# Five dense attentions: stacked q and k through device memory, and a new order of their pipeline

## What is computed

```python
# context_attention_0 (154 keys, a mask row), causal_attention_1 (512 keys, causal)
# remembered_attention_1 (154 keys), context_attention_2 (154 keys, a mask per query)
scores = einsum('bhqd,bhkd->bhqk', q, k) / sqrt(8)       # masked where the part has a mask
out = einsum('bhqk,bhkd->bhqd', softmax(scores), v)
# differential_attention_2 (512 keys): two softmaxes over two pairs of q and k
wei = softmax(q1 @ k1.T / sqrt(8)) - lamb * softmax(q2 @ k2.T / sqrt(8))
```

## Time and profile before

| | us |
|---|---|
| median of 3 runs (5172.68 to 5182.78) | 5179.9 |
| span of the profiled execution | 5172.1 |
| busy: PE, DVE, ACT, POOL | 4078.9, 3239.9, 2680.8, 1243.4 |
| attend, context 0 (482 to 661) | 179 |
| attend, causal (855 to 1120) | 265 |
| attend, remembered (1202 to 1382) | 180 |
| attend, differential, first and second (1529 to 1797, 1799 to 2066) | 268, 267 |
| attend, context 2 (2135 to 2328) | 193 |

### The profile page before, as it was taken

One profiled execution on the slowest core, in us unless ns is written; L12 is line 12 of the kernel. 1 busy time (PEld: TensorE's weight loads), 2 busy tenths in 40 slices (PEclk: granted clock), 3 DMA queues, 4 the chain that ended last, 5 costly groups with the idle time before them and its releaser, 6 DMA issues. The chain is left out here.

```text
span 5172.1 us, 126690 instructions
## 1 busy us (share of the span) xinstructions
PE 4078.9 (79%) x45549; PEld 2392.3 (46%) x45678; DVE 3239.9 (63%) x5957; ACT 2680.8 (52%) x5510; POOL 1243.4 (24%) x2886
## 2 busy tenths in 40 slices
PE   2004767876668888596997579999999999999997
PEld 1003333332332222243443337777777777777775
DVE  7996444544437676534555327777777777777775
ACT  2034723554547667361224436666666666666665
POOL 0011200111201111110000134444444444444443
PEclk6557977987879999796998679999999999999998
DMA  2000020000010000002441000000000000000000
GB/s 57 0 0 1 2 69 23 1 1 1 1 33 2 1 2 1 11 1 57 140 137 51 5 23 28 6 10 24 6 28 6 6 28 6 10 24 6 28 6 11
DMA packets 60833, 110.22 MB, mean 21 GB/s; under 512 B 11399, under 2 KB 43251, under 8 KB 59164
## 3 DMA queue, kind: packets, MB, share of 16 engines
q1 hardware_dynamic: 59558, 101.70, 6.8%
q0 software_dynamic: 784, 1.80, 0.2%
HBM read 96.06 MB, written 1.74 MB: 19 GB/s over the span
## 5 line engine op out<-in xcount | busy, mean ns | idle before, releaser
L676 DVE TENSOR_REDUCE minus_max<-banks 128x1 f32<-128x512 f32 (+4 forms) x1152 | 605.7, 569 | 320.7 <-PE banks L571 314.4
L641 ACT ACTIVATE probs<-banks 128x512 f32<-128x512 f32 (+4 forms) x1152 | 581.1, 557 | 339.0 <-PE banks L609 336.6
L2961 POOL TENSOR_TENSOR loc_cos_part<-loc_cos_part,loc_sin_part 128x512 f32<-128x512 f32 x388 | 494.3, 1274 | 672.0 <-DVE loc_sin_part L3390 671.4
L3034 PE MATMUL banks<-loc_w_qkv,loc_shifted 128*128 128x256 f32 x1552 | 391.4, 395 | 15.4 <-DMA loc_adder_of<-loc_head_ones 15.4
L609 PE MATMUL banks<-q_stack,k_stack 64*128 64x512 bf16 (+3 forms) x1152 | 255.3, 382 | 97.1 <-DMA q_stack<-max_rows 69.6
L3423 DVE TENSOR_TENSOR loc_headsT<-banks,loc_sum_inv 128x512 f32<-128x512 f32 x192 | 132.5, 690 | 291.5 <-ACT loc_sum_inv L3295 291.5
L3034 PEld LDWEIGHTS banks<-loc_w_qkv,loc_shifted 128*128 128x128 f32 x1552 | 282.1, 192 | 55.0 <-DMA loc_w_qkv<-in_L_ffn_Wqkv_dram 15.7
L622 PE MATMUL banks<-probs,pair_rows 128*32 128x512 f32 (+3 forms) x2304 | 295.5, 589 | 0.0
L3415 DVE TENSOR_REDUCE loc_minus_max<-banks 128x4 f32<-128x384 f32 x386 | 196.9, 551 | 153.3 <-PE banks L3101 152.5
L700 POOL CAST max_parts<-minus_max 128x8 bf16<-128x8 f32 x192 | 36.4, 189 | 1043.2 <-DVE minus_max L676 1043.2
L1987 PE MATMUL banks<-identity,srt_b 128*128 128x128 f32 x64 | 11.3, 321 | 344.4 <-DVE srt_b L2267 344.4
(11 more groups left out here) (524 smaller groups left out, 9305.9 us busy)
## 6 DMA issues: line engine op xcount, KB each, us to landing
expert_share<-limited_rows SPq DMA_DIRECT2D x136, 256.0 KB, 3.9
expert_w<-in_L_ffn_pairs_dram SPq DMA_DIRECT2D x84, 192.0 KB, 2.3
loc_w_qkv<-in_L_ffn_Wqkv_dram SPq DMA_DIRECT2D x7, 1536.0 KB, 8.3
expert_share<-grouped_rows SPq DMA_DIRECT2D x32, 256.0 KB, 4.0
q_stack<-max_rows SPq DMA_DIRECT2D x384, 3.0 KB
loc_v_edge<-loc_v SPq DMA_DIRECT2D x192, 32.0 KB, 1.8
fixed_w<-in_L_ffn_experts_dram SPq DMA_DIRECT2D x8, 514.5 KB, 3.7
loc_pack<-in_L_ffn_pack_dram SPq DMA_DIRECT2D x6, 537.5 KB, 4.0
```

Source lines behind the costliest of these rows:

```text
L641: nc.scalar.activation(probs[(a % 2) * C + k][e][0:kn, q0:S], t_bank[e][0:kn, q0:S], ACT.Exp, scale=scale).then_inc(s["exp_done"], 1)
L676: nc.vector.tensor_reduce(minus_max[:, u, e, qs[0]:qs[0] + len(qs)], view, AX.X, ALU.max, negate=True).then_inc(s["max_done"], 1)
L2961: nc.gpsimd.tensor_tensor(cos_part[:, tiles, :], cos_part[:, tiles, :], sin_part[:, tiles, :], ALU.add).then_inc(s["summed"], 1)
L3034: ins = nc.tensor.matmul(g.bank[3 * j][:, (t % 2) * QK:(t % 2 + 1) * QK], xs[:, t * P:(t + 1) * P], w_qkv[:, ds(at, QK)], start=True, stop ...
```

## The change

- A class `Stacks` owns two q and two k stacks of a whole batch (8 pairs each) and, per pair of projections, two tensors in device memory, 128 x 6 x (4 batches of keys or queries), bf16. `store` writes a batch there in six DMAs (pieces repeated as the six slots want them), `load` fetches a batch in four, with heads and slots laid on 48 rows of each half. `project` gains an SP program that stores each batch as it is ready and loads the first two, and a GpSimd program that sets the stacks to 1.0 before. The second q and k of the differential part are stored at its end.
- The selection matrices, their products, the copies to `q_stack` and `k_stack` and the patterns go. A key bias gets its own row by two DMAs per batch; the row of maxima lies behind it.
- `attend` is unrolled for 32 pairs, with no hardware loop. Direct runs 3 pairs ahead (4 with 154 keys), the maxima are sent 2 ahead, from two buffers. Three banks serve the turned scores and three the direct ones. The unit on TensorE is one turned product of half e and one direct product of half 1-e; values come in halves of the queries at set places between the units, turning of rows and heads too. Masks come unit by unit. Products read only the rows and keys that are used (51 or 52 rows, 26 keys in the second key tile).
- SP loads the batch after next when a batch has been used up. GpSimd copies value rows into a double buffer.
- The first part loads neither `select_q` nor `select_k` nor the patterns, and computes no `stack_ones`.

```diff
+    def store(self, sp, i, first, count, sem):
+        q_parts, k_parts = self.parts[i]
+        q_dram, k_dram = self.drams[i]
+        q = slice(first * S, (first + count) * S)
+        k = slice(first * self.nk, (first + count) * self.nk)
+        for slots, pieces in ((slice(0, 3), slice(0, 3)), (slice(3, 5), slice(0, 2)), (slice(5, 6), slice(0, 1))):
+            sp.dma_start(q_dram[:, slots, q], q_parts[:, pieces, q]).then_inc(sem, 16)
+        for slots, piece in ((slice(0, 3), 0), (slice(3, 5), 1), (slice(5, 6), 2)):
+            n = slots.stop - slots.start
+            sp.dma_start(k_dram[:, slots, k], k_parts[:, piece:piece + 1, k].to_broadcast(
+                [P, n, count * self.nk])).then_inc(sem, 16)
+    def load(self, sp, batch):
+        i, b = divmod(batch, B)
+        for e in range(2):
+            rows = slice(64 * e, 64 * e + MAX_ROW)
+            for stacks, dram, n in ((self.q, self.drams[i][0], S), (self.k, self.drams[i][1], self.nk)):
+                src = dram.rearrange("(a e d) s t -> e (d s) a t", e=2, d=DH)[e][:, :, b * n:(b + 1) * n]
+                sp.dma_start(stacks[batch % 2][rows, :, :], src).then_inc(self.s[f"loaded{batch % 2}"], 16)
+    def load_bias(self, sp, batch, key_bias):
+        for e in range(2):
+            row = 64 * e + MAX_ROW
+            src = key_bias[0:1, batch:batch + 1, 0:self.nk].to_broadcast([1, PAIRS, self.nk])
+            sp.dma_start(self.k[batch % 2][row:row + 1, :, :], src).then_inc(self.s[f"bias_loaded{batch % 2}"], 16)
+def project(nc, g, projections, values, stacks):
...
+            @block.sync
+            def _(sp):
+                for b in range(B):
+                    sp.wait_ge(s["third_ready"], b * n + 2)
+                    stacks.store(sp, 0, b, 1, stacks.s[f"stored{b}"])
+                    if b == 0:
+                        sp.wait_ge(stacks.s["stacks_filled"], 4)
+                    if b in (1, 2):
+                        sp.wait_ge(stacks.s[f"stored{b - 1}"], 96)
+                        stacks.load(sp, b - 1)
+                if n > 2:
+                    sp.wait_ge(s["third_ready"], B * n)
+                    stacks.store(sp, 1, 0, B, stacks.s["stored_later"])
+            @block.gpsimd
+            def _(pool):
+                for buffer in (*stacks.k, *stacks.q):
+                    nc.gpsimd.memset(buffer[:, :, :], 1.0).then_inc(stacks.s["stacks_filled"], 1)
...
-    LAG = 2 if n_kt > 2 else 1
-    RING = 4
-    QUAD = PAIRS // 2
+    N, QUADS = B * PAIRS, B * PAIRS // 2
+    AHEAD = 4 if context else 3
+    SENT_AHEAD = 2
+    max_row = stacks.max_row
+    VALUES_OWN = {7: (0, 0)} if context else {13: (0, 0), 14: (0, 1)}
+    VALUES_NEXT = ({1: (0, 1), 2: (1, 0), 3: (1, 1)} if context else
+                   {1: (1, 0), 3: (1, 1), 5: (2, 0), 6: (2, 1), 7: (3, 0), 9: (3, 1)})
+    ROWS_AT = (1, 5) if context else (4, 12)
+    COPY_ROWS_AT = (2, 6) if context else (5, 13)
+    COPY_HEADS_AT = 4 if context else 11
+    TURN_HEADS_AT = 6 if context else 15
 
...
+        def load_next(sp, b):
+
+            batch = which * B + b + 2
+            if batch >= B * len(stacks.parts):
+                return
+            sp.wait_ge(s["turned_ready"], (b + 1) * PAIRS * 2 * C)
+            if batch // B:
+                sp.wait_ge(stacks.s["stored_later"], 96)
+            else:
+                sp.wait_ge(stacks.s[f"stored{batch}"], 96)
+            stacks.load(sp, batch)
...
+                for n in range(N):
+                    sp.wait_ge(s["rows_done"], n + 1)
+                    for e in range(2):
+                        row = 64 * e + max_row
+                        sp.dma_start(stacks.q[batch_of(n) % 2][row:row + 3, n % PAIRS, :],
+                                     max_rows[n % 2][3 * e:3 * e + 3, :]).then_inc(s[f"sent{n % 2}"], 16)
+                    b, a = divmod(n, PAIRS)
+                    if a == 2 and b:
+                        load_next(sp, b - 1)
+                load_next(sp, B - 1)
 
...
+                def turned(n, k, e):
+                    q_stack, k_stack = stacks_of(n)
+                    k0, kn = ktiles[k]
+                    q0 = k0 if causal else 0
+                    rows_e = slice(64 * e, 64 * e + max_row + 3)
+                    if k == 0 and e == 0:
+                        pe.wait_ge(s[f"sent{n % 2}"], 32 * (n // 2 + 1))
+                    if plain:
+                        after(pe, "exp_done", unit(n, k, e) - 2)
+                    nc.tensor.matmul(t_bank(n, k, e)[0:kn, q0:S], k_stack[rows_e, k0:k0 + kn], q_stack[rows_e, q0:S],
+                                     start=plain, stop=True, skip_group_check=True).then_inc(s["turned_ready"], 1)
...
+                def slot(n):
+                    quad = n // 2
+                    ahead = n + AHEAD
                     for k in range(C):
+                        for i in range(2):
+                            if not plain:
+                                turned_masks(n, k, i)
+                                if ahead < N:
+                                    direct_masks(ahead, k, i)
+                            turned(n, k, i)
+                            if ahead < N:
+                                direct(ahead, k, i)
+                            at = place(n, k, i)
+                            if at in VALUES_NEXT and quad:
+                                attend_values(quad - 1, *VALUES_NEXT[at])
+                            if at in VALUES_OWN:
+                                attend_values(quad, *VALUES_OWN[at])
+                            if at in ROWS_AT and n + SENT_AHEAD < N:
+                                turn_rows(n + SENT_AHEAD)
+                            if at == TURN_HEADS_AT and quad:
+                                turn_heads(quad - 1)
+                for n in range(AHEAD):
+                    for k in range(C):
+                        for i in range(2):
+                            if not plain:
+                                direct_masks(n, k, i)
+                            direct(n, k, i)
+                    if 0 < n <= SENT_AHEAD:
+                        turn_rows(n - 1)
+                for n in range(N):
+                    slot(n)
+                for piece in VALUES_NEXT.values():
+                    attend_values(QUADS - 1, *piece)
+                turn_heads(QUADS - 1)
...
+                def exp(n, k, e):
+                    k0, kn = ktiles[k]
+                    q0 = k0 if causal else 0
+                    quad, u = n // 2, n % 2
+                    act.wait_ge(s["turned_ready"], unit(n, k, e) + 1)
+                    after(act, "values_done", (quad - copies[u]) * C + k + 1)
+                    nc.scalar.activation(probs_of(n, k, e)[0:kn, q0:S], t_bank(n, k, e)[0:kn, q0:S], ACT.Exp,
+                                         scale=scale).then_inc(s["exp_done"], 1)
+                def copy_rows(n):
+                    act.wait_ge(s["max_turned"], n + 1)
+                    after(act, f"sent{n % 2}", 32 * (n // 2))
+                    nc.scalar.activation(max_rows[n % 2][0:6, :], x_bank[0:6, :], ACT.Copy).then_inc(s["rows_done"], 1)
+                def copy_heads(quad):
+                    act.wait_ge(s["values_done"], (quad + 1) * C)
+                    after(act, "heads_ready", quad)
+                    nc.scalar.activation(headsT[:, :], o_bank[:, :], ACT.Copy).then_inc(s["headsT_copied"], 1)
+                for n in range(SENT_AHEAD):
+                    copy_rows(n)
+                for n in range(N):
+                    for k in range(C):
+                        for e in range(2):
+                            exp(n, k, e)
+                            at = place(n, k, e)
+                            if at in COPY_ROWS_AT and n + SENT_AHEAD < N:
+                                copy_rows(n + SENT_AHEAD)
+                            if at == COPY_HEADS_AT and n // 2:
+                                copy_heads(n // 2 - 1)
+                copy_heads(QUADS - 1)
...
+                def copy_values(quad):
+                    b, a = divmod(2 * quad, PAIRS)
+                    after(pool, "values_done", (quad - 1) * C)
+                    for u in range(2):
+                        nc.gpsimd.tensor_copy(pair_rows[quad % 2][u][:, :, :, 0:DH + 1],
+                                              tile_rows[:, b * n_kt:(b + 1) * n_kt, (a + u) * 2:(a + u) * 2 + 2, :]
+                                              ).then_inc(s["rows_copied"], 1)
...
-                for dst, name in ((g.select_q[:, :, :], "c_select_q"), (g.select_k[:, :, :], "c_select_k"),
-                                  (g.ones_pattern[:, :], "c_ones_pattern"), (g.max_pattern[:, :], "c_max_pattern"),
-                                  (g.causal_q[:, :], "c_causal_q"), (g.causal_k[:, :], "c_causal_k"),
+                for dst, name in ((g.causal_q[:, :], "c_causal_q"), (g.causal_k[:, :], "c_causal_k"),
                                   (g.band[:, :, :, :], "c_band")):
```

(2 more changed lines are left out.)

552 lines of the change are left out of this document (202 added, 350 removed).

## The result

The changed kernel takes 5256.2 us (5249.1 to 5266.1, 4 runs) beside 5180.1 us (5172.7 to 5182.8) of the kernel before: a ratio of 1.0156, 95% interval 1.0144 to 1.0168. It is slower by 76 us; 240 us less were forecast. The profiled spans are 5264.3 and 5172.1 us, 92.2 apart, because the profiled run of the changed kernel was the longest of its four.

What follows compares the result with a forecast made beforehand. TensorE was taken to lead, never alone. Savings of 86 (contexts), 27 (causal), 118 (differential), 6 (context 2) and 3 (start) make 240 us off the profiled 5172.1: 4932 + 8 = 4940 us, range 4870 to 5060.

Steps and rivals of the forecast that it cites:

- rival D: TensorE's clock: the emptier TensorE stays at half clock in the attentions, 363 us slower, 5540 us; chance 0.05.
- the sum: All stages: product times added per pair at full clock, then savings added over pairs, fills and start: 240 us saved.
- Differential: Both differential attentions: VectorE leads, pairs fall from 7.5 to 5.8 us, 53 us saved in each.
- Later loads: SP queue in the attentions: loads stand before the maxima's DMA twice an attention, costing 1 to 2 us each.
- Causal: Causal attention: TensorE's sum is 6.05 us a pair, 6.5 taken for today's 7.4, 28 us saved.
- Contexts: First and remembered context attentions: floor 3.05, 3.4 us a pair taken, 50 us saved in each.
- Rival B: 26-column products don't overlap their direct partner: 0.2 to 0.3 us per such unit, 46 us, 4985 us; chance 0.10.
- The way through memory: Stacks stored to device memory and loaded back: 1.57 MB each way per batch, 5.4 us a batch.
- the term of project(): SP's stores and loads in project(): 14 us, some 7 past its present end in contexts, 10 to 12 in causal.
- the fills of the five stages: Fills before attentions: 11 us saved before the second differential, 5 before the first, causal and context 2 at 0, key-bias contexts lose 3.
- Rival E: DMA queue: pieces take 0.2 us each instead of 0.055, five stages lose 400 us, 5350 us; chance 0.04.
- The start: Start of the kernel: 1.5 MB of select_q and select_k no longer load, 3 us saved.

Runs made afterwards that it cites:

- e1: Changed kernel plus a 128-row product before every turned score product, 512 columns in the three context attentions, 384 in the causal one: 5356.6 us, ratio 1.0343.
- e2: As e1, but each added product multiplies only 48 rows, with the same 512 or 384 columns: 5589.7 us.
- e7: Changed kernel with added 128-row products only in the first 6 of the 32 pairs of the context and causal attentions: 5263.2 us.
- e15: Changed kernel with late stores, 128-column second context key tile, 64-row turned products, added causal products (384 columns in four pairs, then 192): 4999.6 us, ratio 0.9667.
- late stores alone: Changed kernel with stores after batch 0's and the load of batch 1 moved from the projections to the attention's SP block: 5180.6 us, ratio 1.0007.
- e18: As e15, plus a full product of 128 columns before each turned product in the two context attentions with a key bias: 5057.2 us, ratio 0.9770.

## Why the prediction was wrong

- **The step that failed** is the "against" in rival D: at 79% busy the clock was 0.96, at 87% 1.00, and the new shares are 80 to 93%, so the sum priced every product at full clock. It took the busy share for what the clock follows. The causal attention is busy for 100% at 0.50, and e1 and e2 give 1.00 and 0.50 at the same busy share. D had a chance of 0.05; its mechanism came in four of six attentions. Of the 332 us between the forecast and the profiled spans (240 the one way, 92 the other), 273 lie in the six attentions and 59 outside them. D's prices for a pair at the low clock were about right: 5.3 us for contexts (6.0 and 6.2 where the clock was 0.50), 11.5 for causal (9.6 and 10.6, since the slack of the sum went), 9.4 for context 2 (9.4). It cost 134 us, not 363, as the differential pairs kept their clock and context 2 kept it for most pairs. The page named there, the Trainium skill, TensorE: Matmul & The Clock Gate, section "Part 1: The HAM clock gate", lets TensorE's busy-ness set the clock; the trace contradicts it if busy is read from the busy column (100% at 0.50).
- **Differential**: right. 5.8 us a pair forecast, 5.6 the most frequent, 5.8 and 5.9 the means; 31 x 1.7 = 53 forecast, 52 and 48 measured. VectorE was to be over 90% busy; it is at 82%. Later loads were put at 1 to 2 us each; by the pairs beside them the three in the first attention cost 1.6 to 2.3 us, the two in the second 3 and 6. In the first attention the fill lost 8 where 5 were to be saved; before the second, 11 are saved, as forecast.
- **Causal**: the sum was right, its clock wrong: 6.15 us a pair at full clock in e7 for 6.05 in the sum and 6.5 taken; 9.6 and 10.6 in the changed kernel.
- **Contexts**: 3.4 us a pair forecast. Where the clock is full in e15, pairs of 3.0 and 4.5 alternate, 3.75 on the mean, so even then 11 us too few for each. Rival B is true as well, 0.24 us per narrow unit (0.2 to 0.3 forecast), and with e1's added products the narrow tile also costs the clock (0.52 in both contexts, for 0.88 and 0.76 with the turned product widened). The sum lacks a wait besides. The turned heads go to the bank that the turned maxima use, so ScalarE must have copied the maxima (L768) before TensorE turns the heads (L712), once in two pairs. In order of time, e15:

```profile
549.49 1.05 ACT L762 ACTIVATE probs<-banks 128x512 f32<-128x512 f32 x2
550.45 0.57 ACT L768 ACTIVATE max_rows<-banks 6x512 bf16<-6x512 f32 x1
551.12 0.63 PE L712 MATMUL banks<-identity,headsT 128*128 128x128 f32 x4 [1.86 <-issue]
```

  In the changed kernel this wait is 1.4 to 1.6 us. No run removes it, so what it costs isn't measured.
- **The way through memory**: the term of project() was mis-sized. For the fills of the five stages the prediction took 3, 0, 3, -5 and 0 us (7, 1, 7, -1 and 3 with the later loads); 13, 15, 13, 8 and 16 came. It priced SP's issue at 0.43 us each; in the rows of the fill nine stores took 6.22 + 4.01 + 4.74 = 15 us for 4. A slower issue had been written down as a bound (10.65 us in the earlier trace rows) and then not used. Rival E's 0.2 us a piece isn't it: late stores alone, with as many pieces, give 76 us back.
- **The start**: 3 us forecast, 2.7 measured.
- The sum at full clock wasn't wrong in kind: with the clock and the fills mended, e15 is at 5000 us, inside the range, though it also issues products for nothing. That is another kernel than the one forecast, so it doesn't make the forecast right.

## To carry to other kernels

Before products are taken off TensorE, ask what they did for its clock. The busy share doesn't tell; how many of the 128 rows the products feed told it in the causal attention and in context 2, though not in the two narrow contexts, so read the granted clock stage by stage in a trial. If a stage runs at 0.50 and is busy throughout, a few products of 128 rows that compute nothing can make it faster (causal, 311 to 240 us); where a stage also waits they can make it slower (contexts, 168 to 252 us in e1, 137 to 159 in e18). And work that is queued on an engine in a block's tail delays all engines, whether or not anyone needs it: put it into the next block.
